# Making the second attention's v operand by 64 small products in TensorE instead of a store to and a load from DRAM

## What is computed

```python
def _L0_attn_b_ref(query, qkv_proj, qkv_bias, out_proj, out_bias):
    L, N, E = query.shape            # 32, 256, 128
    qkv = (einsum('lne,fe->lnf', query, qkv_proj) + qkv_bias).reshape(L, N, inner, 3)
    q, k, v = (qkv[..., 0], qkv[..., 1], qkv[..., 2])
    # 16 heads of 8 channels; attention runs over L (32 positions), for each of N*16 pairs
    attn = softmax(SCALE * einsum('bld,bmd->blm', q, k))
    out = einsum('blm,bmd->bld', attn, v)
    return einsum('lni,ei->lne', out, out_proj) + out_bias

x = x + _L0_attn_a_ref(_layernorm(x), ...)     # first layer, heads over 256 positions
x = x + _L0_ffn_ref(_layernorm(x), ...)
x = x + _L0_attn_b_ref(_layernorm(x), ...)     # second layer
x = x + _L0_ffn_ref(_layernorm(x), ...)
```

## Time and profile before

| what | us |
|---|---|
| runs: median, lowest, highest of three | 2331.38, 2323.47, 2338.67 |
| the profiled execution's own time | 2336.02 |
| its span, first to last instruction | 2333.9 |
| the sixteen B passes | from 1249 to about 1968 of the span |

### The profile page before, as it was taken

How to read it: one execution, slowest core, us unless ns; L and a number is a source line. 1 busy time by engine, 2 the same in 40 slices (tenths; PEclk the granted TensorE clock), 3 DMA queues, 4 the chain that set the end, 5 groups by cost and what they waited for, 6 DMA issues and landing times. The chain is left out here.

```text
span 2333.9 us, 39713 instructions
## 1 busy us (share of the span) xinstructions
PE 1794.3 (77%) x10948; PEld 1229.9 (53%) x10948; DVE 1559.8 (67%) x5490; ACT 1238.9 (53%) x2637; POOL 1111.1 (48%) x1591
## 2 busy tenths in 40 slices
PE   4899999999999975999882465664664655899984
PEld 2666666666666653666551343543443543666653
DVE  2899999999999964666562365564564654566653
ACT  2888888889888851333331343443543532333331
POOL 3134333444333343777764244443453444477776
PEclk9999999999999987999995687787787886999997
DMA  4222222222222104877762112122122122678774
GB/s 132 62 74 69 77 75 80 66 85 71 73 78 75 54 25 160 174 176 174 163 138 37 38 53 65 47 56 62 46 58 61 46 63 70 182 170 184 174 164 74
DMA packets 176172, 217.64 MB, mean 93 GB/s; under 512 B 25825, under 2 KB 120290, under 8 KB 173906
## 3 DMA queue, kind: packets, MB, share of 16 engines
q1 hardware_dynamic: 105938, 168.92, 25.1%
q0 software_dynamic: 52352, 37.79, 10.7%
q10 hardware_dynamic: 17664, 8.39, 1.3%
HBM read 122.31 MB, written 59.14 MB: 78 GB/s over the span
## 5 line engine op out<-in xcount | busy, mean ns | idle before, releaser
L834 ACT ACTIVATE z<-z,nm 128x256 f32<-128x256 f32 x1024 | 450.0, 505 | 24.3 <-DVE nm L1003 21.2
L1003 DVE CUSTOM_DVE_ANT_0 z<-bank_S,big 128x256 f32<-128x256 f32 x1024 | 377.5, 419 | 53.1 <-PE bank_S L1292 50.5
L1302 PE MATMUL bank_T<-cst,z 128*128 128x128 f32 x2048 | 308.3, 283 | 9.9 <-ACT z L834 5.0
L722 POOL DMA_INDIRECT regions<-xs,index x256 | 254.6, 995 | 112.8 <-issue 100.4
L748 POOL DMA_INDIRECT x<-yrows,rows x152 | 236.4, 1555 | 115.5 <-issue 110.8
L748 POOL DMA_INDIRECT out_x<-yrows,rows x152 | 235.9, 1552 | 114.2 <-issue 92.7
L1302 PEld LDWEIGHTS bank_T<-cst,z 128*128 128x128 f32 x2048 | 227.3, 142 | 83.5 <-issue 38.1
L469 ACT COPY probT<-bank_T 128x512 f32<-128x512 f32 x448 | 249.2, 578 | 25.8 <-PE bank_T L1302 23.0
L1340 PE MATMUL bank_S<-probT,vw 128*128 128x128 f32 x256 | 55.5, 389 | 246.6 <-ACT vw L825 246.6
L1432 PE MATMUL bank_Y<-hid,wdb 128*128 128x512 f32 (+1 forms) x456 | 235.0, 597 | 1.1 <-DVE hid L1203 1.1
L674 POOL TENSOR_TENSOR h<-h,ctxt 128x64 f32<-128x64 f32 x128 | 41.0, 321 | 398.2 <-DVE ctxt L1018 398.2
(11 more groups left out here) (190 smaller groups left out, 4248.4 us busy)
## 6 DMA issues: line engine op xcount, KB each, us to landing
wb<-w_parts SPq DMA_DIRECT2D x76, 704.0 KB, 4.9
rows<-regions SPq DMA_DIRECT2D x76, 260.0 KB, 2.8
big<-v_dram SPq DMA_DIRECT2D x16, 1024.0 KB
wdb<-in_wd SPq DMA_DIRECT2D x76, 192.0 KB, 5.5
qx<-qk_hi SPq DMA_DIRECT2D x128, 64.0 KB, 2.1
kx<-qk_hi SPq DMA_DIRECT2D x128, 64.0 KB, 2.1
kx<-qk_lo SPq DMA_DIRECT2D x128, 64.0 KB, 2.1
qx<-qk_lo SPq DMA_DIRECT2D x128, 64.0 KB, 2.1
```

The source lines that it names most:

```text
L722: pool.indirect_dma_start(out=regions[:, :], out_offset=bass.IndirectOffsetOnAxis(ap=index[:, k, t:t + 1], axis=0), in_=xs[:, k, t, :], in ...
L834: last = act.activation(zt, zt, ACT.Exp, bias=nm[:, n % NM_RING, t:t + 1], scale=-1.0)
L1003: last = dve.tensor_tensor_reduce(z[:, n % Z_RING, t * SEQ:(t + 1) * SEQ], bank[s][:, t * SEQ:(t + 1) * SEQ], bias_a[:, h, P - P * t:P - P ...
L1302: last = pe.transpose(bank[f"T{n % 2}"][:, c:c + P], z[:, n % Z_RING, t * SEQ + k * P:t * SEQ + (k + 1) * P], ident)
```

## The change

v of the second layer is made in the form that the mix wants. For each spot and each k of 0 to 3, PE multiplies the spot's 32 tokens, as weights, with the 32 columns of Wv that belong to head k of the four groups, and puts the result on the 32 partitions from 32k on: 64 products of 128 x 32 by 128 x 32 a pass, in bank E1. ACT copies from bank E1 into one of two buffers `vw2`, one of which takes the place of `vr` in `big`. `vnew`'s addition, both DMA steps and `v_dram` are gone for layer B. v's bias is added to the context, where ACT copies it to `ctxT` (Identity with a bias in place of Copy). Bank E1 is now free when ACT's copies are done (`v_laid`), so `up.0` and the next `qk.0` wait for that instead of for `v_out`. One more clearing of 128 x 2048 stands between the layers. The B table of `STEADY` is written anew for PE, ACT, DVE and POOL; of SP's list only the load of x is left.

```diff
         "sync": """
-            h3.load.0 h2.vstore.0 h2.vload.0""",
+            h3.load.0""",
...
-    vr = big[:, 2 * SPOTS * D:3 * SPOTS * D]
-    vw = sb("vw", [P, SPOTS, GROUPS, 4, DH])
+    vw2 = [v.rearrange("p (s g h d) -> p s g h d", s=SPOTS, g=GROUPS, h=4)
+           for v in (sb("vw", [P, SPOTS * D])[:, :], big[:, 2 * SPOTS * D:3 * SPOTS * D])]
...
                 elif step == "vcopy":
-                    act.wait_ge(vr_landed, (p.i + 1) * 16)
-                    act.wait_ge(b_mixed, p.before(B_ONLY(TOK)))
+                    act.wait_ge(v_done, p.count(1, 1))
+                    act.wait_ge(b_mixed, p.count(B_ONLY(TOK), -TOK))
                     for k in range(4):
                         r = slice(32 * k, 32 * k + 32)
-                        last = act.activation(vw[r, :, :, k, :], vr[r].rearrange("p (s g h d) -> p s g h d", s=SPOTS, g=GROUPS, d=DH)[:, :, :, k, :],
-                                              ACT.Copy)
+                        src = bank["E1"][r, :].rearrange("p (s g d) -> p s g d", s=SPOTS, g=GROUPS)
+                        last = act.activation(vw2[p.i % 2][r, :, :, k, :], src, ACT.Copy)
                     last.then_inc(v_laid, 1)
...
-                        last = act.activation(ctxT[r, n * P:(n + 1) * P].rearrange("p (j l) -> p j l", j=4), src, ACT.Copy)
+                        last = act.activation(ctxT[r, n * P:(n + 1) * P].rearrange("p (j l) -> p j l", j=4), src, ACT.Identity,
+                                              bias=bcol[r, 2, 0:1])
...
-                    dve.memset(kw[:, :, :, :], 0.0).then_inc(kw_cleared, 1)
+                    dve.memset(kw, 0.0).then_inc(b_cleared, 1)
+                    dve.memset(vw2[1], 0.0).then_inc(b_cleared, 1)
...
+                elif step == "v":
+
+                    pe.wait_ge(qk_out, p.count(2, 1))
+                    w = proj_vo[:, 1, :].rearrange("p (g h d) -> p g h d", g=GROUPS, h=4)
+                    for spot in range(SPOTS):
+                        for k in range(4):
+                            last = pe.matmul(bank["E1"][32 * k:32 * k + 32, 32 * spot:32 * spot + 32],
+                                             xnT[:, 32 * spot:32 * spot + 32], w[:, :, k, :], start=True, stop=True,
+                                             tile_position=(0, 32 * k))
                     last.then_inc(v_done, 1)
...
-                        pe.wait_ge(v_out, p.count(1, 1 if final else 2))
+                        if p.kind == "A":
+                            pe.wait_ge(v_out, p.count(A_ONLY(1), 1 if final else 2))
+                        else:
+                            pe.wait_ge(v_laid, p.count(B_ONLY(1), 1 if final else 2))
```

More of the change, by code:

```diff
@@ L215 @@
         "pe": """
-            h2.qk.1 e0.down.0 h2.v.0 e0.end.0 u2.bscores.0 u2.bscores.1 e1.turn2.0 u2.bscores.2 e1.logits.0
-            e1.gate.0 e1.up.0 u2.bscores.3 e1.gate.1 e1.up.1 u2.bmix.0 e1.gate.2 u2.bmix.1 u2.bmix.2 h3.turn1.0
-            e1.up.2 u2.bmix.3 e1.rank.0 h3.qk.0 u2.bout.0""",
+            e0.up.1 e0.gate.2 u1.bmix.2 e0.up.2 h2.turn1.0 u1.bmix.3 h2.qk.0 e0.rank.0 u1.bout.0 h2.qk.1 e0.down.0
+            u2.bscores.0 e0.end.0 u2.bscores.1 u2.bscores.2 e1.turn2.0 h2.v.0 e1.logits.0 e1.gate.0 u2.bscores.3
@@ L219 @@
+            e1.up.0 u2.bmix.0 e1.gate.1 u2.bmix.1""",
         "act": """
-            e0.gate.0 u1.bscores.2 h1.vcopy.0 e0.gate.1 u1.bscores.3 e0.gate.2 u1.bmix.0 u1.bmix.1 h2.turn1.0
-            u1.bmix.2 u1.bmix.3 h2.qk.0 e0.share.0 h2.qk.1 e0.sum.0 e0.end.0 e1.turn2.0 u2.bscores.0 u2.bscores.1""",
+            h2.qk.0 h2.qk.1 e0.sum.0 e0.end.0 e1.turn2.0 u2.bscores.0 u2.bscores.1 u2.bscores.2 h2.vcopy.0 e1.gate.0
+            e1.gate.1 u2.bscores.3 u2.bmix.0 e1.gate.2 u2.bmix.1 u2.bmix.2 h3.turn1.0 e1.share.0 u2.bmix.3""",
@@ L222 @@
         "dve": """
[L223 to L227, removed]
+            h3.stats1.0 e0.rank.0 e0.share.0 e0.rank.1 e0.rank.2 e0.rank.3 e0.rank.4 u1.bout.0 e1.stats2.0
@@ L228 @@
+            e0.share.1 e0.share.2 e0.share.3 u2.bscores.0 e0.end.0 e1.xn2.0 u2.bscores.1 u2.bscores.2 u2.bsum.0
+            u2.bsum.1 h3.xn1.0 u2.bsum.2 u2.bprobs.0 e1.gate.0 u2.bprobs.1 e1.up.0 u2.bscores.3 u2.bprobs.2
+            e1.gate.1 u2.bsum.3 e1.logits.0 e1.up.1 e1.route.0 e1.gate.2 u2.bprobs.3 e1.up.2 e1.route.1 e1.route.2
+            e1.route.3 e1.route.4""",
         "pool": """
-            e0.rows.0 e1.newton.0 e0.scatter.0 e0.scatter.1 e1.cut2.0 e1.cut2.1 e0.scatter.2 u2.bsum.0 u3.keep.0
@@ L525, in head @@
                             sp.dma_start(dst[c:P:4, n, :].bitcast(F32), src.bitcast(F32)).then_inc(spread_landed[n], 16)
[L527 to L538, removed]
             def experts(p, step, n):
@@ L650, in head @@
                 if step == "vcopy":
-                    pool.wait_ge(v_out, p.count(1, 1))
+                    pool.wait_ge(v_out, p.count(A_ONLY(1), 1))
                     pool.wait_ge(mixed, p.before(CONTEXTS, 2 * GROUPS - 2 * n - 2))
@@ L985, in head @@
                 elif step == "v":
-                    m = "AB".index(p.kind)
                     dve.wait_ge(v_done, p.count(1, 1))
                     dve.wait_ge(v_copied, p.before(A_ONLY(GROUPS)))
-                    if p.kind == "B" and not p.first:
-                        dve.wait_ge(v_stored, p.i * 64)
                     dve.tensor_tensor(vnew[:, :, :], bank["E1"][:, :].rearrange("p (t d) -> p t d", t=TOK),
-                                      spread(bc[:, m * P:(m + 1) * P], 1, TOK), ALU.add).then_inc(v_out, 1)
+                                      spread(bc[:, 0:P], 1, TOK), ALU.add).then_inc(v_out, 1)
             def units(p, step, n):
@@ L1269, in head @@
                         pe.wait_ge(h_ready, p.before(NT, NT))
-                        pe.wait_ge(v_out, p.before(1))
+                        if p.kind == "A":
+                            pe.wait_ge(v_out, p.before(A_ONLY(1)))
+                        else:
+                            pe.wait_ge(v_laid, p.before(B_ONLY(1)))
                     pe.matmul(bank[("E1", "E0")[n]][:, :], proj[:, half, n, :], xnT[:, :], start=True, stop=True
                               ).then_inc(qk_done, 1)
+                elif step == "v" and p.kind == "A":
+                    pe.wait_ge(qk_out, p.count(2, 1))
+                    for t in range(TOK):
+                        last = pe.matmul(bank["E1"][:, t * P:(t + 1) * P], xnT[:, t * P:(t + 1) * P], proj_vo[:, 0, :],
+                                         start=True, stop=True)
+                    last.then_inc(v_done, 1)
                 elif step == "v":
                     pe.wait_ge(qk_out, p.count(2, 1))
-                    for t in range(TOK):
-                        last = pe.matmul(bank["E1"][:, t * P:(t + 1) * P], xnT[:, t * P:(t + 1) * P], proj_vo[:, half, :],
-                                         start=True, stop=True)
+                    w = proj_vo[:, 1, :].rearrange("p (g h d) -> p g h d", g=GROUPS, h=4)
[4 more added lines that the diff above has]
+                                             tile_position=(0, 32 * k))
                     last.then_inc(v_done, 1)
```

32 lines of the change are left out of this document (17 added, 15 removed).

## The result

The changed kernel takes 2107.9 us, the median of four runs (2105.5 to 2109.3), against 2329.8 for the kernel before: a ratio of 0.904, 95% interval 0.901 to 0.908. The forecast was 2147 with a range of 2095 to 2220; the direction and the range held, and the gain was 222 us where 184 had been forecast.

The account below looks back on a forecast made before the run. The B passes were held bound by the wait for v's DRAM load. Terms 19.04 + 2.60 + 1.37 + 5.00 + 0.14 + 2.74 = 30.89 us a pass, 11.55 less than 42.44, 184.8 in 16: 2147, range 2095 to 2220.

Parts of the forecast that it names:

- The bound and its removal: B passes: everybody waits for v's load from DRAM, 246.3 us in 16 waits; without it a pass of 42.44 us takes 27.0.
- The part of the pass that stays: B pass from the end of v's copies to the end of `turn2`, mostly DVE's and ACT's work in turn: 19.04 us.
- what the new order adds: DVE work now behind v's copies, 2.60 us a pass, and scores ahead of the second layer norm, 1.37 us.
- an idle DVE there: Sign of being right: DVE idle between the first transpose and the first gate tile in the B passes.
- only the last four are on the path, 0.2 us: ACT's context copies with a bias: at most 0.05 us more each, four on the path, costed at nothing.
- The products: v's 64 products on PE, right behind `turn2`: 128 pairs at 39 ns, 5.0 us a pass.
- nothing on the path: Lower bound for v's products: hidden whole if ACT's copy of `xf` and POOL's cut of it end last.
- The copies: ACT's four copies of v, now reading PSUM: 2.74 us a pass, against 2.54 from SBUF.
- DVE as the bound: Rival: DVE sets the B pass at layer A's 91% busy share, 25.3 us a pass, time 2058; chance 0.09.
- the 85%: Sign of being wrong: DVE busy for over 85% of a B pass.
- Dear products: Rival: v's products cost 70 ns a pair, v 9.0 us, a pass 34.9, time 2211; chance 0.13.
- The slower case: Rival: v's products take the wait's place, 255 ns a pair, a pass of 58.5 us, time 2588; chance 0.04.

## Why the prediction was right, and where its sum was off

**The bound and its removal.** Right. ACT's wait for the load was everybody's wait: the run with four loads moved the pass by as much as the wait. No DMA is left at the head of the waits.

**The part of the pass that stays, and what the new order adds.** The prediction added 19.04 + 2.60 + 1.37 = 23.01 us from the end of the copies to the end of `turn2`. In the pass shown that is from 1389.88 to 1413.70, 23.82 us. They held as a sum, and that is in part luck, for the path is not the one that was added up. The prediction had DVE wait for ACT's tanh behind the copies, and named an idle DVE there as a sign of being right. In the pass shown DVE works without a pause up to the first gate tile, and the tanh lies ready 1.58 us before DVE comes: POOL's divisions and the layer norm set that stretch. Two things on the real path the prediction missed: the bias, "only the last four are on the path, 0.2 us", is on it with 12 copies and 94 ns each, and the layer norm that the new table puts beside POOL's divisions grew from 1.1 to 2.1 us. Alone they cost 1.3 and 1.5 us a pass, together 1.9, which is more than the 0.8 by which the sum was short.

**The products: the step that failed.** "I take the middle, 39 ns and 5.0 us": v takes 1.30 us, 8.7 ns a record, and ahead of the copies stands ACT's own work, not v. From the end of `turn2` to the start of the copies it is 1413.70 to 1416.20, 2.50 us, against 5.14 in the sum. Both of the rows that set the price misled in the same way. Layer A's 16 products come in rounds of four, one for each column position, and start together within a round; the first round, from the same step as the earlier trace rows:

```profile
300.77 0.13 PEld L1317 LDWEIGHTS bank_O<-probT,vx 128*32 128x32 f32 x4 [0.17 <-ACT probT L469]
300.77 0.42 PE L1317 MATMUL bank_O<-probT,vx 128*32 128x256 f32 x4
```

Four matmuls take 0.42 us and 16 take 1.07, so each further round of four takes 0.22 us, with 256 columns to move. Spread evenly over its products that gave the prediction its 46 ns, and the loads, spread in the same way, their 32. Neither says what a round with 32 columns costs, which is 4 x 8.7 = 35 ns here. That the run with one column position after the other gives 29.5 ns a record, near the 32, is chance. The place on the path failed with the price: up to 3.94 us v costs nothing, so that even at the right size the sum charged it where it is hidden. Of the lower bound, "nothing on the path", the prediction said the right thing and then did not choose it.

The run with v twice over took 2137.8 us with v lasting 4.92, near the 2147 that the prediction worked out for 5.0. That does not confirm the sum. In that run's chain stand v, the gap in it and the router's product at the lower clock, on PE, and not ACT's copies of v (start, us, what):

```profile
1415.61 1.57 PE bank_E L1274 x102
1417.18 2.28 issue
...
1420.47 1.81 PE bank_Y L1360 x8
```

**The copies.** 2.74 charged, 2.38 measured: reading PSUM did not cost more than reading SBUF (2.54).

Together: 0.81 - 2.64 - 0.36 = -2.19 us a pass, 35 us in 16, of the 39 between 2147 and 2108. The errors have both signs, and the largest is the price of v.

**The rivals.** DVE as the bound: not quite, 84% busy where layer A shows 91%. But in the pass shown it is busy 24.53 of 28.70 us, just over the 85% that the prediction named as a sign of being wrong, and the chain runs through DVE and POOL where the prediction saw DVE wait. Dear products: only in rows of 256 records and more, where PE's instructions came late; the changed kernel's rows of 128 have no gap. The slower case has its like in the run with v four times over, where PE's gaps took the place of the wait and 50 of the 222 us were left.

## What to carry to other kernels

When every engine stops for one DMA, look at how many DMA engines that DMA keeps busy before designing it away: here four loads in place of one gave 192 of the 222 us. How the faster load does with the new order of work was not run. Nor was it tried to lay v out by an engine's own copies between groups of 32 partitions. When a table of work is written anew, follow the chain through a whole pass afterwards: the two small things that the change put on it cost 16 and 18 us alone and 25 together. Price small products at different column positions as a group, not each as one, and keep rows of them short: 128 records came without a gap here, 256 mostly not.

## What the runs showed of the hardware that was not expected

- A weight load and matmul of 32 columns at four column positions in turn follow each other every 8.7 ns, at one position every 29.5.
- PE's instructions came in pieces of 16 KB, 256 of them in each. Of a long row of such records 150 to 171 came without a gap (in the first pass some 256); after that PE stood 1.8 to 2.7 us, in the passes shown, and again for each further 128.
- One DMA with 4 outermost in its source had 4 packets in flight, one with 32 outermost 10 to 16.
- A plain copy of 32 x 128 from PSUM took ACT 264 ns, with a bias 358.
